# Cross attention: query sums by VectorE from fp32 projections and split early; turned probabilities loaded ahead of keys; another order at its end

## The reference

```python
# cross attention on the layer-normed x; K = V = ctx (8192 x 1024), its last 512 rows replaced
Q = einsum('bqe,fe->bqf', x, Wq) + bq
K_new = einsum('bqe,fe->bqf', x, Wk) + bk
V_new = einsum('bqe,fe->bqf', x, Wv) + bv
k_cache = dynamic_update_slice(k_cache, K_new, (0, past_kv_len, 0))   # V alike
scores = einsum('bqe,bke->bqk', Q, K) * scale + attention_mask
attn = softmax(scores, axis=-1)
x = x + einsum('bqk,bke->bqe', attn, V)
# then: x = x + self_attention(layernorm(x)); x = x + moe(layernorm(x))
```

## Time and profile before

| | |
|---|---|
| median of 3 runs (lowest, highest) | 1391.89 us (1391.18, 1395.9) |
| the profiled execution, and its span | 1393.09 us, 1391.3 us |
| projections of cross attention | 0 to 153 us |
| its pairs of chunks 0 to 7 | 153 to 815 us |
| its end, up to the first projection of self attention | 815 to 861 us |
| busy: VectorE, ScalarE, GpSimd | 929.5, 716.4, 208.2 us |

### The profile page before, as it was taken

One profiled execution on the slowest core, in us unless ns is written; L12 is line 12 of the kernel. 1 busy time (PEld: TensorE's weight loads), 2 busy tenths in 40 slices (PEclk: granted clock), 3 DMA queues, 4 the chain that ended last, 5 costly groups with the idle time before them and its releaser, 6 DMA issues.

```text
span 1391.3 us, 17591 instructions
## 1 busy us (share of the span) xinstructions
PE 1342.9 (97%) x6228; PEld 1092.6 (79%) x6228; DVE 929.5 (67%) x1412; ACT 716.4 (51%) x1165; POOL 208.2 (15%) x252
## 2 busy tenths in 40 slices
PE   7999889999999999999999988999999999999999
PEld 6878767878878888787788876877777888888887
DVE  6666757567666657757567646686766676777665
ACT  3332435556665656745566652554533435666561
POOL 3003500000000000000000000344422013112023
PEclk9999999999999999999999998999999999999999
DMA  7466355474656657466474452900510456988766
GB/s 248 153 213 230 128 187 181 143 238 137 220 170 204 205 151 258 124 221 198 130 251 137 145 178 72 277 8 31 213 36 31 152 191 210 322 303 296 265 241 214
DMA packets 103032, 254.30 MB, mean 183 GB/s; under 512 B 10097, under 2 KB 56241, under 8 KB 89457
## 3 DMA queue, kind: packets, MB, share of 16 engines
q1 hardware_dynamic: 89280, 194.02, 43.0%
q0 software_dynamic: 10784, 48.93, 10.0%
q10 hardware_dynamic: 2880, 10.22, 1.9%
HBM read 210.67 MB, written 41.42 MB: 181 GB/s over the span
## 4 chain that ended last, share of the span: by engine, by line
PE 79%; DVE 9%; DMA 6%; issue 2%; SPq 2%; ACT 2%; POOL 1%; DVEq 0%; POOLq 0%; ACTq 0%
PE banks L37 21%; PE banks L39 20%; PE banks L38 20%; DMA b_p_in<-pt_dram 6%; PE a_banks L37 3%; PE a_banks L38 3%; PE a_banks L39 3%; PE banks L1184 2%; DVE b_k_lo L1604 2%; PE banks L1155 2%; PE banks L1168 1%; DVE V_lo L1609 1%; SPq L753 1%; DVE b_turned L1661 1%; DVE b_PT_lo L1620 1%
## 5 line engine op out<-in xcount | busy, mean ns | idle before, releaser
L37 PE MATMUL banks<-V_hi,b_PT_hi 128*128 128x512 f32 x512 | 204.1, 399 | 13.6 <-DVE b_PT_lo L1620 13.4
L38 PE MATMUL banks<-V_lo,b_PT_hi 128*128 128x512 f32 x512 | 201.3, 393 | 0.0
L39 PE MATMUL banks<-V_hi,b_PT_lo 128*128 128x512 f32 x512 | 201.1, 393 | 0.0
L37 PEld LDWEIGHTS banks<-V_hi,b_PT_hi 128*128 128x128 f32 x512 | 97.3, 190 | 41.4 <-DVE b_PT_lo L1620 21.7
L1339 ACT ACTIVATE b_PT_hi<-b_p_in 128x512 fp32r<-128x512 f32 x64 | 40.0, 625 | 168.9 <-DMA b_p_in<-pt_dram 168.9
L1620 DVE TENSOR_TENSOR b_PT_lo<-b_p_in,b_PT_hi 128x512 fp32r<-128x512 f32 x64 | 44.1, 689 | 119.5 <-ACT b_PT_hi L1339 119.5
L2712 DVE TENSOR_TENSOR e_lo<-e_raw,e_hi 128x1024 fp32r<-128x1024 f32 x80 | 96.2, 1242 | 33.2 <-ACT e_hi L2539 32.7
L39 PEld LDWEIGHTS banks<-V_hi,b_PT_lo 128*128 128x128 f32 x512 | 97.3, 190 | 20.7
L38 PEld LDWEIGHTS banks<-V_lo,b_PT_hi 128*128 128x128 f32 x512 | 97.5, 191 | 19.8
L839 POOL DMA_DIRECT2D b_s<-mask x32 | 23.2, 725 | 579.0 <-DVE b_turned L1661 576.0
L37 PE MATMUL banks<-b_k_hi,QT_hi 128*128 128x512 f32 x256 | 100.6, 393 | 5.3 <-DVE b_k_lo L1604 5.3
(11 more groups left out here) (359 smaller groups left out, 3269.8 us busy)
## 6 DMA issues: line engine op xcount, KB each, us to landing
b_v_raw<-kv SPq DMA_DIRECT2D x30, 1024.0 KB, 6.0
e_raw<-w_up SPq DMA_DIRECT2D x40, 512.0 KB, 5.0
e_raw<-w_down SPq DMA_DIRECT2D x40, 512.0 KB, 6.3
b_k_raw<-kv SPq DMA_DIRECT2D x19, 1024.0 KB, 5.3
raw<-kv SPq DMA_DIRECT2D x18, 1024.0 KB, 5.4
b_s<-mask POOLq DMA_DIRECT2D x32, 512.0 KB, 7.0
pt_dram<-b_turned SPq DMA_DIRECT2D x64, 256.0 KB, 2.6
b_p_in<-pt_dram SPq DMA_DIRECT2D x256, 64.0 KB, 4.7
```

The costliest lines, as they stand in the source:

```text
L37: pe.matmul(out, lhs_hi, rhs_hi, start=first, stop=False, skip_group_check=onto)
L38: pe.matmul(out, lhs_hi, rhs_lo, start=False, stop=False, skip_group_check=onto)
L39: return pe.matmul(out, lhs_lo, rhs_hi, start=False, stop=last, skip_group_check=onto)
```

## The change

In the projections the biased Q tiles stay in fp32 (in the places of `kraw`), and VectorE makes the four query sums from them in the idle time of groups 2 and 3, and GpSimd none; ScalarE and VectorE split the sums before group 5. VectorE makes the differences of ops 5 and 2 of pair 0 inside group 5, the second of them into a tile of its own (`t2`), so that x2 survives and is neither copied nor loaded again in pair 0. Pair 0 gets its own order for its first half on ScalarE and VectorE. On SyncE's queue each `load_turned` moves up ahead of loads of keys or values. At the end the two weight splits move ahead of steps 59 and 61, `pt_hi(60)` ahead of the last values, `pt_lo(63)` behind `normalize(0)`, and the last `take_rows` behind two splits of x. The diff, cut to its core:

```diff
+        features = (X["kraw"][1], X["kraw"][0])
+        first, second = slice(0, 2 * P), slice(2 * P, 4 * P)
+        sums = (X["q1"], X["q2"], X["q3"], features[0][:, :, first])
+        splits = ((QT_hi[:, 0:4, first], QT_lo[:, 0:4, first]), X["q2_split"], X["q3_split"], X["q4_split"])
+
+        def biased_tile(o):
+            g, i = divmod(o, 4)
+            return tmp[:, o % 2, :] if g < 2 else features[g - 2][:, i, :]
+
+        def split_part(o, x):
+            return x[:, second] if o // 4 == 2 else x
...
-            q = lambda x, f, t: x[:, 4 * f:4 * f + 4, 2 * t * P:(2 * t + 2) * P]
-            done = X["combined"]
-            q3, q1, q2, q4 = X["q3"], X["q1"], X["q2"], X["q4"]
-            pool.wait_ge(out_lo, 4 * DB // 2)
-            pool.wait_ge(low_ready, 16)
-            for x, f, t in ((q3, 0, 0), (q1, 1, 0), (q2, 0, 1), (q4, 1, 1)):
-                pool.tensor_tensor(x[:, :, :], f32(q(QT_hi, f, t)), f32(q(QT_lo, f, t)), ALU.add).then_inc(done, 1)
-            pool.wait_ge(done, 4)
-            pool.tensor_tensor(q1[:, :, :], q1[:, :, :], q3[:, :, :], ALU.add).then_inc(done, 1)
-            pool.wait_ge(done, 5)
-            pool.tensor_tensor(q3[:, :, :], q2[:, :, :], q3[:, :, :], ALU.subtract).then_inc(done, 1)
-            pool.wait_ge(done, 6)
-            pool.tensor_tensor(q2[:, :, :], q1[:, :, :], q2[:, :, :], ALU.subtract).then_inc(done, 1)
-            pool.wait_ge(done, 7)
-            pool.tensor_tensor(q4[:, :, :], q4[:, :, :], q2[:, :, :], ALU.subtract).then_inc(done, 1)
...
+            def queries_hi(k):
+                act.wait_ge(summed, (2, 3, 1, 4)[k])
+                if k in (1, 2):
+                    act.wait_ge(weff_stored, 128)
+                if k == 3:
+                    act.wait_ge(out_lo, 4 * DB // 2 + 3)
+                act.activation(splits[k][0][:, :, :], sums[k][:, :, :], ACT.Copy).then_inc(out_hi, 1)
...
+                if g == 4:
+                    queries_hi(0)
                 if 2 * g + 3 < HALVES:
                     weights_hi(2 * g + 3)
+            queries_hi(1)
+            queries_hi(2)
+            queries_hi(3)
...
+            def sum_queries(k):
+                f0, f1 = features
+                s1, s2, s3, s4 = sums
+                out, in0, in1, op = ((s3, f0[:, :, second], f0[:, :, first], ALU.subtract),
+                                     (s1, f1[:, :, first], f0[:, :, first], ALU.add),
+                                     (s2, s1, f0[:, :, second], ALU.subtract),
+                                     (s4, f1[:, :, second], s2, ALU.subtract))[k]
+                dve.wait_ge(biased, 12 if k == 0 else 16)
+                if k:
+                    dve.wait_ge(summed, k)
+                dve.tensor_tensor(out[:, :, :], in0[:, :, :], in1[:, :, :], op).then_inc(summed, 1)
+
+            def queries_lo(k):
+                dve.wait_ge(out_hi, 4 * DB // 2 + k + 1)
+                if k == 3:
+                    dve.wait_ge(out_lo, 4 * DB // 2 + 1)
+                dve.tensor_tensor(splits[k][1][:, :, :], sums[k][:, :, :], f32(splits[k][0][:, :, :]),
+                                  ALU.subtract).then_inc(out_lo, 1)
+
+            def first_difference(h):
+                y, x = raw[:, 0, :].rearrange("p (e n) -> p e n", n=W), X["kraw"][0]
+                es = slice(2 * h, 2 * h + 2)
+                dve.wait_ge(w_split, HALVES + 4 + h)
+                dve.wait_ge(raw_loaded[0], 112)
+                dve.tensor_tensor(x[:, es, :], y[:, es, :], x[:, es, :], ALU.subtract).then_inc(prepared, 1)
+
+            def second_difference(h):
+                y, x = raw[:, 1, :].rearrange("p (e n) -> p e n", n=W), X["kraw"][0]
+                es = slice(2 * h, 2 * h + 2)
+                dve.wait_ge(prepared, h + 1)
+                dve.wait_ge(raw_loaded[1], 112)
+                dve.tensor_tensor(X["t2"][:, es, :], y[:, es, :], x[:, es, :], ALU.subtract).then_inc(prepared, 1)
...
                 if g == 5:
+                    for k in range(4):
+                        queries_lo(k)
                     for h in range(2):
                         dve.wait_ge(w_hi_done, HALVES + 4 + h)
                         dve.tensor_tensor(X["k_lo"][:, h, :, :], X["kraw"][0][:, 2 * h:2 * h + 2, :],
                                           f32(X["k_hi"][:, h, :, :]), ALU.subtract).then_inc(w_split, 1)
+                    first_difference(0)
+                    first_difference(1)
...
-                    if 2 <= o < 16:
+                    if 2 <= o < 8:
                         dve.wait_ge(out_lo, o - 1)
+                    if o == 8:
+                        dve.wait_ge(low_done, LOW_SPLIT)
+                    if o == 16:
+                        dve.wait_ge(summed, 4)
+                    if o == 20:
+                        dve.wait_ge(out_lo, 20)
+                        dve.wait_ge(summed, 4)
...
-                        op = dve.tensor_scalar(tmp[:, o % 2, :], psum, b_cols[:, o - 8:o - 7], SCALE,
+                        op = dve.tensor_scalar(biased_tile(o), psum, b_cols[:, o - 8:o - 7], SCALE,
...
-                        dve.tensor_tensor(out_tile(o, False), tmp[:, o % 2, :], f32(out_tile(o, True)),
-                                          ALU.subtract).then_inc(out_lo, 1)
+                        dve.tensor_tensor(split_part(o, out_tile(o, False)), split_part(o, biased_tile(o)),
+                                          f32(split_part(o, out_tile(o, True))), ALU.subtract).then_inc(out_lo, 1)
+                    if o == 21:
+                        second_difference(0)
+                    if o == 22:
+                        second_difference(1)
...
+                if g == 2:
+                    sum_queries(0)
+                if g == 3:
+                    sum_queries(1)
+                    sum_queries(2)
+                    sum_queries(3)
...
         def keys_raw(j):
 
             s_, i, h = key_half(j)
-            x = raw_of({0: "x1", 1: "x2", 2: "x2", 3: "y1", 4: "x2", 5: "x1", 6: "y2"}[i], s_)
+            x = X["t2"] if i == 2 and s_ == 0 else raw_of({0: "x1", 1: "x2", 2: "x2", 3: "y1", 4: "x2", 5: "x1", 6: "y2"}[i], s_)
...
                 if vh >= 3:
                     sp.wait_ge(b["v_split"], vh - 2)
                 else:
-                    sp.wait_ge(b["prepared"], prepared_keys(0, 4, 1))
+                    sp.wait_ge(own["out_ready"], 24)
                 sp.dma_start(v_raw[:, :, :].rearrange("p k n -> p (k n)"),
                              ins["kv"][4 * (kc - 1) + 2 + h]).then_inc(v_loaded, 16)
 
@@ -762,15 +817,16 @@
                     load_turned(n - 3)
                     load_turned(n - 2)
                     load_values(4 * s_ + 1)
+                    load_turned(n - 1)
                 store_turned(n)
                 store_turned(n + 1)
+                load_turned(n)
                 sp.wait_ge(split_done, split + 8)
...
                 if s_:
                     load_key("x2_again", s_)
-                    load_turned(n - 1)
-                load_turned(n)
+                load_turned(n + 1)
                 if not last:
-                    sp.wait_ge(b["prepared"], prepared_keys(s_, 4, 1))
+                    sp.wait_ge(prepared, prepared_keys(s_, 4, 1))
                     load_key("x2", s_ + 1)
                     sp.wait_ge(split_done, split + 10)
                     load_key("x1", s_ + 1)
...
                 load_values(4 * s_ + 2)
-                load_turned(n + 1)
                 store_turned(n + 2)
                 store_turned(n + 3)
+                load_turned(n + 2)
+                load_turned(n + 3)
                 if not last:
                     sp.wait_ge(split_done, split + 12)
                     load_key("y1", s_ + 1)
-                load_turned(n + 2)
...
                 store_turned(n + 5)
+                load_turned(n + 4)
                 load_values(4 * s_ + 3)
-                load_turned(n + 3)
                 store_turned(n + 6)
-                load_turned(n + 4)
                 store_turned(n + 7)
...
-            sp.wait_ge(own["out_ready"], 24)
-            sp.wait_ge(own["biased"], 24)
-            sp.dma_start(v_raw[:, :, :].rearrange("p k n -> p (k n)"),
-                         raws[1][:, :, :].rearrange("p e n -> p (e n)")).then_inc(v_loaded, 16)
             for s_ in range(PAIRS_OF_CHUNKS):
                 pair_of_chunks(s_)
             load_turned(STEPS - 3)
             load_rows(0)
             load_turned(STEPS - 2)
+            load_turned(STEPS - 1)
             load_rows(1)
-            load_turned(STEPS - 1)
...
                             if i == 0 and s_ == 0:
                                 pe.wait_ge(own["biased"], 20)
+                                pe.wait_ge(own["out_lo"], 20)
...
-                        act.wait_ge(own["biased"], 24)
+                        act.wait_ge(own["biased"], 22 + 2 * h)
...
-            def pair_of_chunks(s_):
+            def first_half():
+                keys_hi(2)
```

(100 more changed lines are left out.)

146 lines of the change are left out of this document (53 added, 93 removed).

## The result

The changed kernel took 1349.88 us in the median of four runs (1348.98 to 1351.05), the kernel before 1391.96 (1391.18 to 1395.9): a ratio of 0.9693, 95% interval 0.9673 to 0.9713. The profiled execution took 1351.05 us with a span of 1349.3, against 1393.09 and 1391.3 before: 42.0 us less of span.

The account below looks back on a forecast made before the run. TensorE, busy 1342.9 of 1391.3 us, was taken as the bound; gains 13.5 + 11.9 + 15.3 = 40.7 us off 1393.1 gave 1352.4, less 1.2 for the median 1351.2, forecast as 1352; range 1347 to 1363.

Parts of the forecast that it names:

- The term for low clock: Pair 0, after the gap before product 3: one stretch at the lower clock, costing 1.7 us.
- the rest of the span: TensorE's time after the second projection: forecast gain 0.
- What bounds it: Whole kernel: TensorE busy 1342.9 of 1391.3 us, so only its idle time and low-clock time can be given back.
- Query sums at 0: Projections: VectorE's query sums cost 0, with 7 us in hand before product 0, kept at 153.11.
- Pair 0: First stretch, 18.9 us of excess: 5.4 stays, including a 3.3 us gap before product 3; gain 13.5, bounds 9.7 to 18.2.
- Probabilities ahead: Pair 1 to the last pair's product: probability transfers issued before 1 MB loads gain 11.9 of 12.4 us, 0.5 left for restarts.
- The end: Last product to second projection: reordered splits gain 15.3 of 16.2 us; step 60's second half costs 0.1, third turn 0.8.
- the mask: Rival, pair 0: mask lands after 9.1 us instead of 4.1, delaying product 4; 3.9 us less gain, 1356 us, chance 0.13.
- Exchange: Rival, steady pairs: probabilities land early but something else is just in time; half of 11.9 stays, 1358 us, chance 0.14.
- a tight end: Rival, end: ScalarE's and VectorE's order too tight, step 60's second half or probabilities 63 late; 1358 us, chance 0.11.
- SyncE's queue holding up y1: Rival, every pair: y1's load waits for probabilities n+3, making differences late; 1396 us or more, slower or the same 0.03.
- its point of decision: Pair's end: y1's load delay matters from 13 us on, its time in hand before the difference.

Follow-up runs that it names:

- the two delays tried: Changed kernel with the next pair's y1 load behind step n+4's probability transfers (11.4 us later), 1348.22 us, or behind step n+7's store (16.5 us later), 1388.31 us.
- the two dearest runs: Changed kernel with only step n+3's probability transfers behind the pair's last values, 1381.94 us; changed kernel with y1's load behind step n+7's store, 1388.31 us.

## Why the prediction was right

1352 us was forecast and 1349.9 measured, with the mechanism right in each of its parts. The term for low clock was right by luck, and the rest of the span is open:

- *What bounds it.* Only TensorE's idle and slow time could be given back. True: 16.0 us of busy time (low clock and long restarts) and 26 of idle.
- *Query sums at 0.* Right, with the cover shown: 3.3 us added on VectorE cost nothing. The forecast kept product 0 at 153.11; it came 0.6 earlier. Much of that may be scatter: in the nine other profiles with the same projections it starts between 152.34 and 153.10, and in the two with the old ones at 152.78 and 153.24.
- *Pair 0.* 14.5 against 13.5. Products 1 and 2 follow without a gap, and the gap before product 3 was 2.49 instead of 3.3. The 1.7 of low clock behind it came, but the reason given for it (it had followed gaps of 2.05 us and more, and not one of 1.92) doesn't hold: the same gap has it in five of nine profiles. This term was luck. VectorE's waits for ScalarE were 1.24 us ahead of key half 4's split and 0.88 ahead of half 6's, where I had 1.3 and 1.1, and the first split waited 0.40, where I had 0.6 with the semaphores. That is 0.5 of the 0.8 us; the other 0.3 is the queue's own work, 15.3 us instead of 15.6. That the queue makes this gap, and not TensorE's banks, was shown by reading them early.
- *Probabilities ahead.* 12.6 against 11.9, and 10.5 came back when six pairs were undone. The half microsecond left for restarts wasn't needed: the pairs are free of gaps.
- *The end.* 15.4 against 15.3: step 60's second half didn't wait, and the third turn began at 817.32, 0.3 us behind the matmul before it instead of 0.8.
- *The rest.* Taken as unchanged; it was 1.1 longer, within what this part differs by between profiles (528.3 to 531.0), for a reason that is open.

Of the rivals, the mask's mechanism exists (shown by turning the tiles late), but it landed in time: 5.0 us after its issue at 170.95, 0.9 more than forecast. Exchange and a tight end didn't occur. The one I gave least to, SyncE's queue holding up y1, is the dearest: its point of decision, put at 13 us, lies between the two delays tried. Where my expectations failed (32.1 against 7.7 us, 38.4 against 6), both had the same fault. I had priced the moved transfer by its own lateness and not by what stands behind it: on SyncE the transfers after a wait, on VectorE the splits after a difference.

A faster version came out of it: the changed kernel with product 2's banks read early, 1346.24 us in the median, each of its times below each of the changed kernel's.

## What to carry to other kernels

Where a group of small transfers and a 1 MB load share a queue, ask which of them an engine waits for next, and put that first; but count what is queued behind every wait that the move places on the queue, since here one wait put ahead of a load turned a loss of 11 us into one of 32. Work out an engine's queue up to the one instruction that releases TensorE, and order by that, as an engine's last read before a bank is reused is as much a release as a split. An early load's slack is used up at a point: bracket it by delaying the load in two sizes.

## What was not expected of the hardware

The low clock after a stall is not a fixed price. Nine of the profiled executions have the same gap of 2.48 or 2.49 us before product 3; in five a stretch of 3.4 us at 1.2 GHz followed (the changed kernel's is shown above), in four none did. The run with SyncE's old order, behind its gap of 2.49:

```profile
173.40:176.80 3.40, 3.40 (x17) 2.81 (x16) 0.60 (x2) 1.06 (x1) 0.00 (x0) 1.00 1.04 263
```

17 matmuls were started in 3.40 us here and 10 there. Of the 14 stalls between 2.26 and 4.25 us in the two dearest runs, ten were followed by low clock, all seven of 3.4 us and more among them, and four weren't, the longest of these 3.23 us; behind gaps of 1.86 us and less in the pairs none was seen. Below 2 us it is no different: SyncE's order and the end's on the kernel before has gaps of 1.90 and 1.92 us in pair 0, and low clock came with the first matmul after the one and 1.3 us after the other, while the same gap of 1.92 in the kernel before has none, nor has one of 2.01 in the run with SyncE's order alone. Behind the gap of 1.90:

```profile
167.60:171.00 3.40, 3.40 (x8) 2.63 (x9) 3.19 (x9) 2.42 (x5) 0.00 (x0) 0.53 0.03 13
```

So here a stall of 1.9 to 3.3 us cost its length and either nothing or 1.7 us. The spread between runs of one kernel goes the same way (mean clock 1.0 at 1348.98 us, 0.997 at 1351.05).

GpSimd's sums slowed VectorE's subtractions by very different factors: 5.57 us and 3.92 us against 2.29 for the weight split, both beside GpSimd. The sums of the kernel before add two different tiles, those of the experiment one tile to itself; whether that is the reason wasn't tried.
